# First stage of a graph layer: transposes ahead of the build, value sums ahead of weights, and ScalarE instead of GpSimd for one widening copy

## The chip, the cores and the metric

One core of one Trainium2 chip. The time is that of the whole program on the device, in microseconds (us). Engines: TensorE (PE in profiles, its weight loads PEld), VectorE (DVE), ScalarE (ACT), GpSimd (POOL), SyncE (SP, which only issues transfers here).

## The reference, cut to what matters

A layer on a graph of 3125 nodes and 53125 edges sorted by destination. Node features `x` (3125 x 256) are normalized to `xn`, and then:

```
h = spmm(xn)                       # sum over edges of weight * xn[dst], into row src
z = spmm(h);  a0 = softmax(z @ W0.T + b0);  z = spmm([a0, a0]);  a1 = softmax(z @ W1.T + b1)
x = x + tanh(concat(a0, a1) + h) + mix(xn)    # mix: linear attention, k and v = layernorm(xn @ wk.T), (xn @ wv.T)
x = x + ffn(layernorm(x))                     # 8 experts, top 1, fixed capacity
```

The kernel never gathers edges. It turns the edge list into the dense adjacency matrix (25 x 25 tiles of 128 x 128) by matrix products of one-hot rows, stores it, and applies it three times. The change lies in the first stage, where edges are sorted into tiles, keys and values are projected, and the first strip of the matrix is built.

## The kernel before, in words

Each engine runs one list of instructions in order; engines wait for each other at semaphores. A loop of `it` = 0, 1, ... is written out on four engines. For `it` up to 24 it handles one tile of 128 nodes per pass and, a few passes later, one *unit* (four 128 x 128 blocks of the matrix: rows of tile u, columns of tiles 0 to 3). These first 25 passes are the first stage. What stands in pass `it`:

- **TensorE**, in this order: `product(it)` (keys and values of a node tile, L1654), `ranks(it)` (three matmuls that count edges per slot, L1628 to L1630), `build(it-3)` (the blocks of a unit, L1676), `slots(it-1)` (18 matmuls that put a tile's edges into slots, L1640), `kvprod(it-5)` (L1661), `turn(it+1)` (two transposes of the next node tile for the next `product`, L1587), `apply(it-4)` (a unit times the features, L1697).
- **ScalarE**: `turned(it)` (L819, the transposed tile from PSUM to `XT`), `weigh(it-3)` (L848, the unit's four row one-hots times their edge weights), in passes 1, 5 and 15 `cast` (L813 to L815), `normal(it+3)` (L806), in every fifth pass a square root of head variances (L898), `paired(it)` (L836), `squares(it)` (L825 copies the product out, L828 sums squares per head), `evac(it-3)` (L861, the built unit from PSUM; after every fifth unit it also issues a store, L865), `kept(it-1)` (L840, the slots' records from PSUM to `recs`).
- **VectorE**: in passes 2, 6 and 16 `prepare` (a group of tiles' edge fields), `spread(it)` (L1105, and the scan L1107), in every fifth pass `head_var` (L1129, waits for `squares(it-1)`), `slot(it-1)` (L1114 reads the ranks, L1117 makes one-hots, L1122 the payload), in every fifth pass `head_scale` (L1134 to L1138, waits for ScalarE's root), `normed(it-5)` (L1145), `hots(it-2)` (L1165, a unit's row and column one-hots `eq_b` in bf16).
- **GpSimd**: in passes 1, 5 and 15 `pieces` (L686 to L690), weights of tile it-1 out of `recs` (L700, L702, semaphore `s_wsum`), the value sum of tile it-6 (L707, `s_vsum`), and the widening of unit it-2's column one-hots from bf16 to f32, `lead_col` (L712, semaphore `s_wide`). L702 and L707 add, L712 copies 128 x 512 elements.

One PSUM bank, `MISC`, holds the slots' records in its first part and the transposed tile in its second; the semaphores around it are `s_slotted` and `s_recrd` (`kept` done), `s_turned` and `s_xt` (`turned` done). From pass 25 on, VectorE builds the one-hots alone in bf16, and a pass on TensorE is `build` and `apply`.

Of the kernel before, what the change touches and what calls it, by code (L numbers as in the profile page):

```python
# [18 lines left out]
P = 128  # L19
NT = 25  # L20
# [40 lines left out]
LEAD = NT  # L61
# [65 lines left out]
def hot_free(u):  # L127
    return u - 2 if u < LEAD + 3 else u - 3


KV_LAG = 5
# [18 lines left out]
def graph_program(nc, a, out):  # L150
    ctx = ExitStack()
    with ctx:
# [3 lines left out]
        def sem(name):  # L156
            return ctx.enter_context(nc.semaphore(name))
# [230 lines left out]
        s_eq = sem("s_eq")  # L388
        s_hot = sem("s_hot")
        s_wgt = sem("s_wgt")  # L390
        s_wide = sem("s_wide")
        s_bmm = sem("s_bmm")
        s_bev = sem("s_bev")
        s_app = sem("s_app")
# [256 lines left out]
        def _(gp):  # L651
# [40 lines left out]
            for it in range(NT + KV_LAG + 1):  # L692
                if it in CAST_AT:
                    pieces(CAST_AT[it])
                if 1 <= it <= NT:
                    j = it - 1
                    w1, w2, w3 = (recs[:, j, 0:6:5, f, :] for f in (2, 3, 4))
                    whole = lead_w[:, j * 8:(j + 1) * 8].rearrange("p (g q) -> p g q", g=2)
                    gp.wait_ge(s_recrd, j + 1)
                    gp.tensor_tensor(whole, w1, w2, ALU.add).then_inc(s_wpart, 1)  # L700
                    gp.wait_ge(s_wpart, j + 1)
                    gp.tensor_tensor(whole, whole, w3, ALU.add).then_inc(s_wsum, 1)  # L702
                if it > KV_LAG:
                    m = it - KV_LAG - 1
                    gp.wait_ge(s_khat, m + 1)
                    ge(gp, s_vsum, m)
                    gp.tensor_tensor(vacc.rearrange("p (c n) -> p c n", c=2), vacc.rearrange("p (c n) -> p c n", c=2), khat[m % 2][:, 2:4, 0:P], ALU.add).then_inc(s_vsum, 1)  # L707
                u = it - HOT_IT
                if 0 <= u < LEAD:
                    gp.wait_ge(s_hot, u + 1)  # L710
                    ge(gp, s_bmm, hot_free(u))
                    gp.tensor_copy(lead_col[hot_of(u)], eq_b[u % 2][:, 1].rearrange("p c k i -> p c i k")).then_inc(s_wide, 1)  # L712

            gp.wait_ge(s_m, 1)
            gp.memset(blank, 0.0).then_inc(s_blank, 1)
# [57 lines left out]
        def _(act):  # L773
# [47 lines left out]
            def squares(m):  # L821
                g, i = m // KT, m % KT
                act.wait_ge(s_prod, m + 1)
                ge(act, s_khat, m - 5)
                nc.scalar.copy(KC[m % 6], ps[:, PROD, :])  # L825
                ge(act, s_sq, m)
                for h in range(NH):
                    head = nc.scalar.activation(sq[:, h * HD:(h + 1) * HD], ps[:, PROD, h * HD:(h + 1) * HD], ACT.Square,  # L828
                                                accum_out=hvar[:, g % 2, i * NH + h:i * NH + h + 1])
                head.then_inc(s_sq, 1)  # L830
# [11 lines left out]
            def weigh(u):  # L842
                act.wait_ge(s_hot, u + 1)
                act.wait_ge(s_wsum, u + 1)
                ge(act, s_bmm, hot_free(u))
                h = hot_of(u)
                for i, (j, s) in enumerate(UNITS[u]):
                    last = nc.scalar.activation(lead_row[h][:, i // 2, i % 2, :], eq_b[u % 2][:, 0, i // 2, :, i % 2], ACT.Copy, scale=lead_w[:, j * 8 + s:j * 8 + s + 1])  # L848
                    if j == s:
                        own = nc.scalar.activation(lead_own[h][:, 0, :], lead_own[h][:, 0, :], ACT.Copy, scale=lead_w[:, j * 8 + 7:j * 8 + 8])  # L850
                        last = own
                last.then_inc(s_wgt, 1)
# [26 lines left out]
            x_rows(2)  # L879
            x_rows(3)  # L880
            for it in range(NU + 3):
                if it < NT:
                    turned(it)
                if it == 1:
                    for to, src in ((wo_n, half("L0_mix_wo")), (wq_n, half("L0_mix_wq")), (W0_n, a["L0_gnn_W0"]),
                                    (W1_n, a["L0_gnn_W1"]), (b1_n, a["L0_ffn_b1"])):
                        act.dma_start(to, src).then_inc(s_wt5, 16)
                u = it - BUILD_IT
                if 0 <= u < LEAD:
                    weigh(u)  # L890
                if it in CAST_AT:
                    cast(CAST_AT[it])
                if it + 3 < NT:
                    normal(it + 3)
                if it in range(KT, NT + 1, KT):
                    g = it // KT - 1
                    act.wait_ge(s_hvar, g + 1)
                    nc.scalar.activation(hrs[:, g % 2, :], hvar[:, g % 2, :], ACT.Sqrt).then_inc(s_hroot, 1)  # L898
                if it < NT:
                    paired(it)  # L900
                    squares(it)
                if it == 2:
                    roots(1)
                if 0 <= u < NU:
                    evac(u)
                    if u - 1 in [strip_end(k) for k in range(NS)]:
                        strip_out(strip_of(u - 1))
                if 1 <= it <= NT:
                    kept(it - 1)
                if it == 2:  # L910
                    others_out()
# [92 lines left out]
        def _(dve):  # L1004
# [143 lines left out]
            def hots(u):  # L1148
# [6 lines left out]
                if u < LEAD:  # L1155
# [4 lines left out]
                        for a in range(2):  # L1160
                            v.tensor_scalar(lead_own[h][:, a, :], iota_n[:, :], rec(t, SPARE, a), None, ALU.is_equal)
                    ge(dve, s_wgt, u - 1)
                    ge(dve, s_wide, u - 1)
                    fields = recs[:, j, 0, 0:2, :].rearrange("p f (c i) -> p f c i", i=2)
                    v.tensor_tensor(eq_b[u % 2], every.unsqueeze(1).unsqueeze(1).to_broadcast([P, 2, 2, P, 2]),  # L1165
                                    fields.unsqueeze(3).to_broadcast([P, 2, 2, P, 2]), ALU.is_equal).then_inc(s_hot, 1)
# [417 lines left out]
        def _(pe):  # L1584
# [47 lines left out]
            def slots(j):  # L1632

                b = j % 2
                k = ohk[b].rearrange("p (c k i) -> p c k i", k=P, i=2)
                p = V[:, b, :].rearrange("p (c f s i) -> p c f s i", f=5, s=NR, i=2)
                pe.wait_ge(s_pay, j + 1)
                ge(pe, s_recrd, j)
                for c in range(WC):
                    last = nc.tensor.matmul(ps[:, MISC, 0:140].rearrange("p (f s) -> p f s", f=5)[:, :, 0:NR], k[:, c // 2, :, c % 2], p[:, c // 2, :, :, c % 2], start=(c == 0), stop=(c == WC - 1))  # L1640
                last.then_inc(s_slotted, 1)

            def turn(m):
                pe.wait_ge(s_xn, m + 1)
                ge(pe, s_xt, m)
                ge(pe, s_recrd, m - 1)
                flip(ps[:, MISC, D:D + P], XN[:, m, 0:P])
                flip(ps[:, MISC, D + P:2 * D], XN[:, m, P:2 * P]).then_inc(s_turned, 1)

# [14 lines left out]
            def build(u):  # L1664
# [2 lines left out]
                piece = lambda a, i, w: pair_b[h][:, a, i // 2, 0:w, i % 2]  # L1667
                ge(pe, s_bev, u - 1)
                pe.wait_ge(s_wgt if u < LEAD else s_hot, u + 1)
                if u < LEAD:  # L1670
                    pe.wait_ge(s_wide, u + 1)
                for i, (j, s) in enumerate(UNITS[u]):
                    c = width(t for _, t in UNITS[u][:i])
                    w = width([s])
# [50 lines left out]
            for it in range(NU + 4):  # L1725
                if it < NT:
                    product(it)
                if it < NT:
                    ranks(it)
                if it == 2:  # L1730
                    others()
                if it == APPLY_IT:
# [10 lines left out]
                    slots(it - 1)  # L1743
                if KV_LAG <= it < NT + KV_LAG:
                    kvprod(it - KV_LAG)
                if it + 1 < NT:
                    turn(it + 1)
                if it == NT + KV_LAG:
                    pe.wait_ge(s_vsum, NT)
                    pe.wait_ge(s_sq, NT)  # L1750
# [260 lines left out]
```

## Time and profile before

| | us |
|---|---|
| median of 3 runs (lowest, highest) | 1113.7 (1112.21, 1114.81) |
| profiled execution, its own time | 1114.14 |
| span of its profile | 1112.4 |
| TensorE busy in the span | 1063.1 (96%) |
| VectorE busy | 716.0 (64%) |
| ScalarE busy | 313.7 (28%) |
| GpSimd busy | 199.1 (18%) |

The shares are means over the whole program; the first stage ends near 212 us. In a row of the timeline the first number is the start in us from the beginning of the span, the second the duration; a bracket at the end gives the idle time of the engine before the row and what ended it. A matmul's start in the timeline can lie up to 0.2 us before its place in the chain of waits, since matmuls overlap.

### The profile page before, as it was taken

How to read it: one execution, taken by the hardware profiler on the slowest of the kernel's cores; microseconds unless marked ns; L12 is line 12 of the kernel's file. 1: busy time of each engine (PE TensorE's matmuls, PEld its weight loads, DVE VectorE, ACT ScalarE, POOL GpSimd, SP SyncE). 2: the span in 40 equal slices, each digit the busy share in tenths (PEclk: the TensorE clock that was granted, in tenths of full speed). 3: DMA queues.
4: the chain of work that ended last, by engine and by line, in shares of the span. 5: the costliest groups of instructions: out<-in, count | busy, mean ns of one | idle time of the engine just before them, and what ended most of it. 6: DMA issues, size and time to landing. Idle time of an engine off the chain costs nothing.

```text
span 1112.4 us, 15255 instructions
## 1 busy us (share of the span) xinstructions
PE 1063.1 (96%) x5391; PEld 664.0 (60%) x5391; DVE 716.0 (64%) x1611; ACT 313.7 (28%) x1042; POOL 199.1 (18%) x243
## 2 busy tenths in 40 slices
PE   5899999999999999999999999999998899999995
PEld 3466566666566665566784444644457566666664
DVE  8999999897775876869840111237777554444444
ACT  4777777322212222222211111211112221222220
POOL 2234454400101010110000000000443511111111
PEclk9999999999999999999999999999999999999998
DMA  6120011123333333423259988897994686555510
GB/s 178 19 58 13 37 49 48 49 95 134 133 134 133 134 133 133 166 110 143 96 203 365 366 311 304 342 329 280 311 323 156 184 223 142 134 134 138 140 39 8
DMA packets 80986, 178.58 MB, mean 161 GB/s; under 512 B 35678, under 2 KB 64122, under 8 KB 68750
## 3 DMA queue, kind: packets, MB, share of 16 engines
q1 hardware_dynamic: 67592, 123.39, 34.8%
q10 hardware_dynamic: 9190, 46.12, 10.5%
q0 software_dynamic: 4128, 8.08, 2.1%
q8 instruction: 45, 0.74, 0.3%
q14 instruction: 31, 0.25, 0.1%
HBM read 116.23 MB, written 63.77 MB: 162 GB/s over the span
## 4 chain that ended last, share of the span: by engine, by line
PE 83%; DVE 9%; ACT 3%; issue 2%; another core or an unknown queue 1%; DMA 1%; POOL 0%; SPq 0%; ACTq 0%; POOLq 0%; DVEq 0%
PE ps L1697 23%; PE ps L1851 20%; PE ps L1976 10%; PE ps L1964 9%; PE ps L1681 7%; PE ps L1654 2%; PE ps L1720 2%; PE ps L1587 2%; PE ps L1640 2%; PE ps L1676 1%; ACT W L828 1%; DVE XT L1487 1%; DVE W L1122 1%; PE ps L1661 1%
## 5 line engine op out<-in xcount | busy, mean ns | idle before, releaser
L1697 PE MATMUL ps<-RING,XX 128*128 128x512 f32 (+2 forms) x700 | 296.2, 548 | 1.6 <-DVE W L1194 1.6
L1851 PE MATMUL ps<-RING,RY 128*128 128x512 f32 (+4 forms) x750 | 271.3, 518 | 1.4 <-issue 1.4
L1851 PEld LDWEIGHTS ps<-RING,RY 128*128 128x128 f32 x750 | 135.0, 192 | 121.3 <-issue 113.6
L861 ACT COPY RING<-ps 128x512 f32<-128x512 f32 (+3 forms) x163 | 92.3, 566 | 279.0 <-PE ps L1681 259.7
L1697 PEld LDWEIGHTS ps<-RING,XX 128*128 128x128 f32 x700 | 117.5, 190 | 68.9 <-issue 61.6
L1187 DVE TENSOR_TENSOR RING<-RING,RY 128x1536 bf16<-128x1536 bf16 (+1 forms) x150 | 140.0, 940 | 4.0
L1681 PEld LDWEIGHTS ps<-RING 128*128 128x128 bf16 x1575 | 100.6, 97 | 52.0 <-issue 46.4
L1177 DVE TENSOR_TENSOR RING<-iota_p,RY 128x1024 bf16<-128x1024 bf16 (+1 forms) x150 | 96.8, 652 | 29.0 <-PE ps L1681 26.5
L1681 PE MATMUL ps<-RING 128*128 128x128 bf16 (+1 forms) x1575 | 112.9, 217 | 0.0
L998 ACT ACTIVATE RY<-ps,b1T 128x489 f32<-128x489 f32 x64 | 42.8, 669 | 164.9 <-PE ps L1964 162.0
L1554 DVE SCALAR_TENSOR_TENSOR W<-ps,RING,W 128x256 f32<-128x256 f32 (+1 forms) x32 | 15.5, 484 | 90.8 <-PE ps L1976 89.7
L1365 DVE TENSOR_REDUCE nmx<-ps 128x4 f32<-128x512 f32 (+2 forms) x7 | 4.4, 634 | 103.8 <-PE ps L1587 103.8
L724 POOL TENSOR_TENSOR XX<-XX,bo_b 128x256 f32<-128x256 f32 x25 | 27.5, 1100 | 232.9 <-PE ps L1681 232.8
L768 POOL DMA_INDIRECT out<-W,RING x32 | 31.3, 979 | 182.2 <-DVE W L1561 160.1
L1976 PE MATMUL ps<-XT,RY 128*128 128x256 f32 (+1 forms) x256 | 55.9, 379 | 0.0
L1976 PE MATMUL ps<-RING,RY 128*128 128x256 f32 (+1 forms) x256 | 55.9, 379 | 0.0
L1964 PE MATMUL ps<-RING,XT 128*128 128x489 f32 x128 | 53.3, 574 | 0.0
L1964 PE MATMUL ps<-RING 128*128 128x489 f32 x128 | 53.1, 573 | 0.0
L1654 PE MATMUL ps<-wkvT,XT 128*128 128x512 f32 x100 | 48.7, 611 | 4.5 <-ACT XT L819 4.5
L1976 PEld LDWEIGHTS ps<-XT,RY 128*128 128x128 f32 (+1 forms) x256 | 47.4, 185 | 9.3 <-issue 1.8
L1976 PEld LDWEIGHTS ps<-RING,RY 128*128 128x128 f32 (+1 forms) x256 | 47.4, 185 | 9.3 <-issue 1.8
L743 POOL DMA_INDIRECT xbuf_dram<-XX,sidx x25 | 25.1, 1003 | 118.9 <-DVE sidx L1475 112.1
(287 smaller groups left out, 1332.5 us busy)
## 6 DMA issues: line engine op xcount, KB each, us to landing
RING<-adj_dram SPq DMA_DIRECT2D x60, 1280.0 KB
adj_dram<-RING ACTq DMA_DIRECT2D x30, 1280.0 KB, 4.8
rbuf_dram<-W SPq DMA_DIRECT2D x8, 516.0 KB, 5.2
RING<-rbuf_dram SPq DMA_DIRECT2D x8, 516.0 KB, 4.0
xbuf_dram<-W SPq DMA_DIRECT2D x8, 512.0 KB, 3.3
XT<-in_L_ffn_w SPq DMA_DIRECT2D x16, 256.0 KB
XT<-in_L_ffn_w SPq DMA_DIRECT2D x4, 1024.0 KB
RING<-in_L_ffn_w SPq DMA_DIRECT2D x16, 256.0 KB
```

What stands on the lines that cost most here:

```text
L724: gp.tensor_tensor(X1[:, j, :], X1[:, j, :], bo_b[:, :], ALU.add).then_inc(s_bo, 1)
L768: gp.indirect_dma_start(out[:, :], bass.IndirectOffsetOnAxis(ap=rbs[0:n, e % 2, c, D + 1:RES].bitcast(I32), axis=0), ybs[0:n, e % 2, c, :] ...
L861: nc.scalar.copy(RING[:, n % 2, at:at + w], ps[:, u % 2, 0:w]).then_inc(s_bev, 1)
L998: nc.scalar.activation(hmT[:, f, 0:CAPX], ps[:, 2 + f % 3, 0:CAPX], ACT.Relu, bias=b1T[:, f, e:e + 1]).then_inc(s_hidv, 1)
L1177: last = v.tensor_tensor(to[:, 0:4:3], every.unsqueeze(1).unsqueeze(1).to_broadcast([P, 2, c, P, 2]), fields[:, 0:2].unsqueeze(3).to_broad ...
L1187: last = v.tensor_tensor(to[:, 1:4], to[:, 3:4].to_broadcast([P, 3, c, P, 2]), fields[:, 2:5].unsqueeze(3).to_broadcast([P, 3, c, P, 2]), ...
L1654: last = nc.tensor.matmul(ps[:, PROD, :], XT[:, c, m * P:(m + 1) * P], wkvT[:, c, :], start=(c == 0), stop=(c == 1))
L1681: last = nc.tensor.matmul(o[:, c:c + w], piece(0, i, P), piece(1 + f, i, w), start=(f == 0), stop=(f == 2 and j != s))
L1697: last = nc.tensor.matmul(ps[:, ACC + dd, 0:w], XN[:, j, dd * H:(dd + 1) * H], at[:, i * w:(i + 1) * w], start=(j == 0), stop=True, skip_g ...
L1851: last = nc.tensor.matmul(o, (Y if l == 0 else S0)[:, j, :], RING[:, slot_of[g % 5], i * across + first:i * across + first + w], start=(j ...
L1964: last = nc.tensor.matmul(ps[:, 2 + f % 3, 0:CAPX], w1s[s][:, c, f * P:(f + 1) * P], xbT[:, s, c, 0:CAPX], start=(c == 0), stop=(c == 1))
L1976: last = nc.tensor.matmul(o, hmT[:, f, c * P:c * P + n], w2s[s][:, f, :], start=(f == 0), stop=(f == 7))
```

## The change

Four edits. (1) On TensorE `turn(it+1)` stands behind `ranks(it)` instead of behind `kvprod`; it waits for the records of one tile earlier (`s_recrd` m-2 instead of m-1), and `slots(it-1)` gets a wait for `turned(it+1)`, because both use `MISC`. (2) On ScalarE `turned(it+1)` moves from the head of the next pass into `squares(it)`, behind the copy L825. (3) On GpSimd the value sum stands ahead of the weights. (4) The widening copy leaves GpSimd and becomes the first instruction of `weigh` on ScalarE; `s_wide` goes, on VectorE and TensorE too.

```
@@ gpsimd, loop over it
                 if it in CAST_AT:
                     pieces(CAST_AT[it])
+                if it > KV_LAG:
+                    m = it - KV_LAG - 1
+                    gp.wait_ge(s_khat, m + 1)
+                    ge(gp, s_vsum, m)
+                    gp.tensor_tensor(vacc..., vacc..., khat[m % 2][:, 2:4, 0:P], ALU.add).then_inc(s_vsum, 1)
                 if 1 <= it <= NT:
...
-                if it > KV_LAG:
...
-                u = it - HOT_IT
-                if 0 <= u < LEAD:
-                    gp.wait_ge(s_hot, u + 1)
-                    ge(gp, s_bmm, hot_free(u))
-                    gp.tensor_copy(lead_col[hot_of(u)], eq_b[u % 2][:, 1].rearrange("p c k i -> p c i k")).then_inc(s_wide, 1)
@@ scalar, squares(m)
                 nc.scalar.copy(KC[m % 6], ps[:, PROD, :])
+                if m + 1 < NT:
+                    turned(m + 1)
@@ scalar, weigh(u)
                 h = hot_of(u)
+                nc.scalar.copy(lead_col[h], eq_b[u % 2][:, 1].rearrange("p c k i -> p c i k"))
                 for i, (j, s) in enumerate(UNITS[u]):
@@ scalar, loop over it
-                if it < NT:
-                    turned(it)
+                if it == 0:
+                    turned(0)
@@ vector, hots(u)
                     ge(dve, s_wgt, u - 1)
-                    ge(dve, s_wide, u - 1)
@@ tensor, slots(j)
                 ge(pe, s_recrd, j)
+                pe.wait_ge(s_xt, min(j + 3, NT))
@@ tensor, turn(m)
                 ge(pe, s_xt, m)
-                ge(pe, s_recrd, m - 1)
+                ge(pe, s_recrd, m - 2)
@@ tensor, build(u)
-                if u < LEAD:
-                    pe.wait_ge(s_wide, u + 1)
@@ tensor, loop over it
                 if it < NT:
                     ranks(it)
+                if it + 1 < NT:
+                    turn(it + 1)
...
                     kvprod(it - KV_LAG)
-                if it + 1 < NT:
-                    turn(it + 1)
```

TensorE, one whole pass of the steady part, before, from `product` to `apply`:

```order
L1654 MATMUL ps<-wkvT,XT 128x512 x2
L1628 MATMUL ps<-HB,before 128x468
L1629 MATMUL ps<-HB,ident_b 128x468
L1630 MATMUL ps<-HB,own_b 128x468
L1676 MATMUL ps<-RING 128x128 x4
L1640 MATMUL ps<-W,RY 128x5x26 x18
L1661 MATMUL ps<-W 128x129 x2
L1587 MATMUL ps<-ident,XX 128x128 x2
L1697 MATMUL ps<-RING,XX 128x512 x2
```

The same pass now (line numbers are those of the changed kernel):

```order
L1651 MATMUL ps<-wkvT,XT 128x512 x2
L1624 MATMUL ps<-HB,before 128x468
L1625 MATMUL ps<-HB,ident_b 128x468
L1626 MATMUL ps<-HB,own_b 128x468
L1583 MATMUL ps<-ident,XX 128x128 x2
L1671 MATMUL ps<-RING 128x128 x4
L1637 MATMUL ps<-W,RY 128x5x26 x18
L1658 MATMUL ps<-W 128x129 x2
L1692 MATMUL ps<-RING,XX 128x512 x2
```

The two transposes (`ps<-ident,XX`) have moved past the build, the slots and `kvprod`; nothing else has changed place.

ScalarE, one pass of the steady part, before, from `turned` to `kept`:

```order
L819 COPY XT<-ps 128x2x128
L848 ACTIVATE RING<-RING,RY 128x128 x4
L806 ACTIVATE XX<-XX,mvx,lnr 128x256
L836 COPY HB<-HB 128x26x9x2
L825 COPY RING<-ps 128x512
L828 ACTIVATE W,hvar<-ps 128x64 x8
L861 COPY RING<-ps 128x512
L840 CAST RY<-ps 128x140
```

And now:

```order
L843 CAST RING<-RING 128x512
L845 ACTIVATE RING<-RING,RY 128x128 x4
L800 ACTIVATE XX<-XX,mvx,lnr 128x256
L832 COPY HB<-HB 128x26x9x2
L819 COPY RING<-ps 128x512
L813 COPY XT<-ps 128x2x128
L824 ACTIVATE W,hvar<-ps 128x64 x8
L858 COPY RING<-ps 128x512
L836 CAST RY<-ps 128x140
```

The copy to `XT` now stands between the copy of the product and the squares, and a cast of 128 x 512 (the widening) opens the pass.

GpSimd around pass 15, before (the three `HB<-HB` rows are `pieces`):

```order
L712 CAST RING<-RING 128x512 [waits s_bmm,s_hot]
L686 TENSOR_TENSOR HB<-HB 128x162 [waits s_cast]
L688 CAST HB<-HB 128x81x2 [waits s_piece]
L690 TENSOR_TENSOR HB<-HB 128x81x2 [waits s_piece]
L700 TENSOR_TENSOR RY<-RY 128x8 [waits s_recrd]
L702 TENSOR_TENSOR RY<-RY 128x8 [waits s_wpart]
L707 TENSOR_TENSOR RY<-RY,W 128x256 [waits s_vsum,s_khat]
```

And now:

```order
L685 TENSOR_TENSOR HB<-HB 128x162 [waits s_cast]
L687 CAST HB<-HB 128x81x2 [waits s_piece]
L689 TENSOR_TENSOR HB<-HB 128x81x2 [waits s_piece]
L698 TENSOR_TENSOR RY<-RY,W 128x256 [waits s_vsum,s_khat]
L704 TENSOR_TENSOR RY<-RY 128x8 [waits s_recrd]
L706 TENSOR_TENSOR RY<-RY 128x8 [waits s_wpart]
```

The value sum (`RY<-RY,W`) no longer stands behind a wait for `s_recrd`, and the widening is gone.

## Rows read from the trace of the kernel before

**Rows 1.** Busy time of each engine in three stretches (start:end, length, busy by engine)

```profile
20.00:60.00 40.00, 31.28 (x191) 19.59 (x192) 38.81 (x84) 28.23 (x142) 8.78 (x20) 0.91 0.23 37
216.00:850.00 634.00, 629.47 (x3315) 375.48 (x3315) 385.06 (x894) 116.66 (x269) 55.02 (x54) 1.00 0.56 208
```

**Rows 2.** Chain that ended last, one pass near 90 us (start, us, what)

```profile
89.67 1.72 PE ps L1697 x4
91.39 1.72 PE ps L1654 x4
93.10 0.20 PE ps L1628
...
93.70 0.89 PE ps L1676 x8
94.59 1.08 PE ps L1640 x18
95.67 0.50 PE ps L1661 x4
...
96.17 0.41 PE ps L1587 x2
```

**Rows 3.** TensorE's waits, 65 to 216 us (us in total, times, longest)

```profile
PE ps L1676 <- POOL RING L712: 2.2, 1, 2.2
PE ps L1587 <- ACT RY L840: 2.1, 4, 0.5
PE ps L1640 <- DVE W L1122: 1.7, 2, 0.9
PE ps L1628 <- DVE HB L1114: 1.5, 1, 1.5
```

**Rows 4.** Timeline of ScalarE behind the issue of a store

```profile
110.09 0.28 ACT L840 CAST RY<-ps 128x140 bf16<-128x140 f32 x1 [0.42 <-ACT RING L861]
```

**Rows 5.** Timeline of ScalarE in a steady pass

```profile
103.53 0.37 ACT L819 COPY XT<-ps 128x256 f32<-128x256 f32 x1 [0.59 <-PE ps L1587]
...
105.47 0.63 ACT L836 COPY HB<-HB 128x468 bf16<-128x468 bf16 x1
106.96 0.59 ACT L825 COPY RING<-ps 128x512 f32<-128x512 f32 x1 [0.87 <-PE ps L1654]
```

**Rows 6.** Timeline of GpSimd and VectorE: a value sum, a payload, and one whole VectorE pass

```profile
89.63 1.82 POOL L707 TENSOR_TENSOR RY<-RY,W 128x256 f32<-128x256 f32 x1
...
90.82 1.86 DVE L1122 TENSOR_TENSOR W<-HB 128x2340 bf16<-128x2340 bf16 x1
...
108.81 1.13 DVE L1107 TENSOR_TENSOR_SCAN HB<-HB 128x468 bf16<-128x468 bf16 x1
...
113.81 1.00 DVE L1145 TENSOR_TENSOR W<-RING,hrs 128x512 f32<-128x512 f32 x1 [0.65 <-POOL RY L707]
...
115.76 1.13 DVE L1107 TENSOR_TENSOR_SCAN HB<-HB 128x468 bf16<-128x468 bf16 x1
```

**Rows 7.** Timeline of TensorE and VectorE around passes 14 to 16

```profile
119.39 1.88 PE L1654 MATMUL ps<-wkvT,XT 128*128 128x512 f32 x4
...
123.75 0.16 DVE L1129 TENSOR_SCALAR hvar<-hvar 128x40 f32<-128x40 f32 x1
...
127.66 0.40 DVE L1134 RECIPROCAL hta<-hrs 128x40 f32<-128x40 f32 x1 [0.52 <-ACT hrs L898]
...
134.82 1.13 DVE L1107 TENSOR_TENSOR_SCAN HB<-HB 128x468 bf16<-128x468 bf16 x1
...
137.80 1.37 DVE L1122 TENSOR_TENSOR W<-HB 128x2340 bf16<-128x2340 bf16 x1
```

**Rows 8.** Timeline of TensorE and VectorE at the end of the stage, passes 24 and 25

```profile
198.54 1.38 DVE L1122 TENSOR_TENSOR W<-HB 128x2340 bf16<-128x2340 bf16 x1
...
201.76 0.69 DVE L1145 TENSOR_TENSOR W<-RING,hrs 128x512 f32<-128x512 f32 x1
...
203.22 0.66 PE L1661 MATMUL ps<-W 128*128 128x129 f32 x4
```

More of the change, by code:

```diff
@@ L390, in graph_program @@
         s_wgt = sem("s_wgt")
-        s_wide = sem("s_wide")
         s_bmm = sem("s_bmm")
@@ L694, in _ @@
                     pieces(CAST_AT[it])
+                if it > KV_LAG:
+                    m = it - KV_LAG - 1
+                    gp.wait_ge(s_khat, m + 1)
+                    ge(gp, s_vsum, m)
+                    gp.tensor_tensor(vacc.rearrange("p (c n) -> p c n", c=2), vacc.rearrange("p (c n) -> p c n", c=2), khat[m % 2][:, 2:4, 0:P], ALU.add).then_inc(s_vsum, 1)
                 if 1 <= it <= NT:
@@ L702, in _ @@
                     gp.tensor_tensor(whole, whole, w3, ALU.add).then_inc(s_wsum, 1)
-                if it > KV_LAG:
[L704 to L707, printed above, removed]
-                u = it - HOT_IT
-                if 0 <= u < LEAD:
-                    gp.wait_ge(s_hot, u + 1)
-                    ge(gp, s_bmm, hot_free(u))
-                    gp.tensor_copy(lead_col[hot_of(u)], eq_b[u % 2][:, 1].rearrange("p c k i -> p c i k")).then_inc(s_wide, 1)
             gp.wait_ge(s_m, 1)
```

## Prediction

> **What bounds the kernel now.** I read four views in this order: busy time by stretch, the chain that ended last, TensorE's waits, and the timeline around the longest of them.
>
> Busy time by stretch divides the program in three. From 20 to 60 us VectorE is busy 38.81 of 40 us while TensorE is busy 31.28: there VectorE sets the pace. From 216 to 850 us TensorE is busy 629.47 of 634 us [rows 1], so whatever the first stage saves or loses is handed on whole to the end. The change can only win between about 60 and 216 us.
>
> The chain of one pass near 90 us lies on TensorE alone: 1.72 (`apply`) + 1.72 (`product`) + 3 x 0.20 (`ranks`) + 0.89 (`build`) + 1.08 (`slots`) + 0.50 (`kvprod`) + 0.41 (`turn`) = 6.92 us [rows 2]. The change leaves that sum as it is; it can only take away waits. Between 65 and 216 us these are 2.2 + 2.1 + 1.7 + 1.5 = 7.5 us [rows 3], which bounds the gain from above. They are of three kinds: four times 0.5 us at `turn`, which waits for `kept`; 1.7 and 1.5 us for VectorE, in two places, pass 6 and pass 16, where `prepare` has lengthened its pass; and once 2.2 us for GpSimd's widening at the end of the stage.
>
> **Edits 1 and 2, the turn.** The four waits of 0.5 us come where `kept` stands behind the issue of a store and waits 0.42 us more [rows 4]. Now `turn(it+1)` waits for `kept` of one tile earlier, which ended a pass ago, so all four go: 2.1 us at most. Stores come every fifth pass, so two of the four lie before pass 16 (7 and 12) and two behind it (17 and 22). What the edit costs: `slots` now needs the copy of `turned`. After the product's end `ranks` and `turn` take 0.6 + 0.41 = 1.0 us, the copy to `XT` is 0.37 us [rows 5], so it is there at about 1.5 us. TensorE reaches `slots` at 0.6 + 0.41 + 0.89 = 1.9 us: covered by the build, with 0.4 us to spare. Without that cover each pass would lose up to the whole copy.
>
> The wait of pass 6 (the 0.8 us that the two in the list leave beside the longest, 0.9) stands at `slots(5)`. The payload that it waits for comes from VectorE, which has no gap there, so its time stays. But the 0.41 us of `turn` now run inside this wait instead of behind it: TensorE starts `product(7)` **0.4 us** earlier.
>
> **Edit 4, the widening on ScalarE.** ScalarE's nearest row is a permuted copy of 468 bf16 elements, 0.63 us [rows 5]; with the overlap of neighbours it holds the engine some 0.5 us, and I take 0.55. In a steady pass ScalarE is idle 0.59 + 0.87 = 1.46 us [rows 5], so it fits, with 0.9 us left, 0.5 where a store is issued. Bounds: nothing, and 1.82 us, the longest GpSimd instruction shown [rows 6], if ScalarE were that slow (I give this little: a copy of 128 x 512 from PSUM takes ScalarE 0.59 us [rows 5]).
>
> **Edit 3 and VectorE's pace.** A VectorE pass without disturbance: from scan to scan 115.76 - 108.81 = 6.95 us, less the 0.65 us that it waits for the value sum, less 0.31 by which `normed` is long there (1.00 against 0.69) [rows 6, 8], gives 6.0 us. A value sum that meets VectorE's work costs the instruction behind it 0.48 us (the payload at 90.82 took 1.86 us, with 1.38 elsewhere, while the sum ended at 91.45) [rows 6, 8]. Before, a pass paid for a value sum and for a widening; now only for the sum, which comes just behind `normed` and so meets `hots` and `spread`. `head_scale` adds some 1.8 us in five passes (payload's end 199.92 to `normed` 201.76) [rows 8]. So VectorE needs 6.0 + 0.48 + 0.36 = 6.84 us against TensorE's 6.92. TensorE keeps the pace, but with little to spare: the sum holds as long as a value sum costs VectorE under 0.56 us in a pass.
>
> **Pass 16.** By then TensorE is 0.4 + 2 x 0.5 = 1.4 us ahead of before Can it keep this? `prepare` makes it wait twice (1.5 and 0.9 us), so VectorE sets the time there. VectorE in turn waited 0.52 us for ScalarE's root at 127.66, which is 6.4 us after the end of `product(14)` at 121.27 [rows 7]. On that path ScalarE now has the widening more (0.55); the wait for `turn` only changes its place. So the root comes 1.4 - 0.55 = 0.85 us earlier, and with it scan and payload (137.80 + 1.37 = 139.17 before), and `slots(15)`. Behind `slots` there is no `turn` any more: 0.41. That gives 1.26 us at `product(17)`. Between reciprocal and scan lie 7.16 us [rows 7] in which GpSimd's widenings no longer disturb VectorE; this is worth between 0 and 2 x 0.48 us, and I take 0.25, since the `pieces` still stand there. Sum up to `product(17)`: **1.5 us** (1.25 to 2.2). In other words: of the 1.4 us collected nothing is added here, because the root moves with the product.
>
> **Passes 17 to 24**: the other two waits at `turn`, **1.0 us**.
>
> **End of the stage.** The 2.2 us at `build(22)` come because the widening stands on GpSimd behind a value sum. On ScalarE it follows `kept(23)`, 0.28 us, and with `weigh`'s four rows (under 1.6 us, since `turned` at 103.53 and `paired` at 105.47 leave 1.94 for more than that [rows 5]) it is done at most 2.4 us behind `slots(23)`; TensorE meanwhile has `kvprod` and `apply`, 0.50 + 1.72 = 2.2 us. So this wait goes but for 0.2 us. What is late next: `kvprod(20)`. It started at 203.22; without the wait TensorE would be there at 201.0. But it needs `normed(20)`, which ended at 202.45, after a payload that ended at 199.92, a `head_scale` and 0.69 us [rows 8]. VectorE did not stand behind the 2.2 us, so this chain does not move by itself: 203.22 - 202.5 = 0.7 us. If `head_scale` shrinks by what GpSimd took, it is up to 1.1. I take **0.9 us**.
>
> **The sum.** 1.5 + 1.0 + 0.9 = 3.4 us. Against the profiled execution: 1114.1 - 3.4 = 1110.7 us. That execution is 0.4 us above the median of the runs shown, so the forecast is 1110.3 us. A change under 0.2% (2.2 us) is about what a measurement of this kernel can't tell from none.
>
> **The rivals.**
>
> *A. The value sum costs VectorE more, and VectorE takes over the pace (slower).* Place: `hots`, `spread` and scan behind `normed`. If each value sum lengthens two instructions instead of one, it costs 0.96 us; VectorE then needs 7.32 us a pass, 0.40 over TensorE, in the 17 passes from 7 to 24 that is 6.8 us. 3.4 are won, so 3.4 us slower: 1117.1. The change turns into a loss from 0.56 + 3.4 / 17 = 0.76 us a pass. For it: the margin is only 0.08 us. Against it: the scan has 1.13 us in every row shown [rows 6, 7], disturbed or not. The Trainium skill, "GPSIMD Engine Reference", section 1 "Specifications", says that GpSimd shares its SBUF interfaces with VectorE, with contention where a VectorE instruction reads two SBUF inputs. All the instructions behind `normed` are of that kind, so by that rule the cost moves with the value sum and does not go. The rows agree as far as the payload goes, and no row bears out two hits by one sum. Chance 0.07.
>
> *B. Less is won.* The root of pass 15 is later than I take it (widening and cast stand in a row ahead of it), so that of the 1.4 us only the 0.4 of `turn` remains, and at the end `kvprod` gains nothing. Then 0.4 + 1.0 = 1.4 us, up to 2.2: about 1112.0. For it: both places hang on chains that TensorE's reordering does not shorten. Chance 0.19.
>
> *C. More is won.* VectorE, freed of the widening, gets far enough ahead that the 2.4 us of pass 16 and the 2.2 us of the end both shrink to little. The upper bound is 7.5 us; with half of pass 16 and 2.0 at the end it is 1.4 + 0.4 + 1.2 + 1.0 + 2.0 = 6.0 us: 1107.7. Against it: the two waits for ScalarE (root, `squares`) tie VectorE to the product. Chance 0.08.
>
> *D. ScalarE becomes the bound (slower).* If the widening held it over the 1.46 us that it is idle, `turned` would be late and `slots` with it. From 1.46 + 3.4 / 17 = 1.66 us on the gain is gone; at 1.82 us it would be 17 x 0.36 = 6.1 us more than forecast, 1116.4. Against it: no ScalarE row of this size is half as slow. Chance 0.02.
>
> **How the numbers follow.** My forecast, 2.3 to 5 us won, has the remaining 0.64. Its own range is 1108.6 to 1111.5. Faster by over 0.2%: 0.64, C's 0.08 and a small part of B, 0.02: 0.74. Within 0.2%: the rest of B, 0.17. Slower: A and D, 0.09. The range takes in C's 1107.7 below and B's 1112.0 with some of the runs' own scatter (2.6 us between lowest and highest) above, and leaves A and D out: 1107.5 to 1112.8.
>
> **What would show it.** Right: no wait of TensorE for `kept` at `turn` between 65 and 200 us; passes 8 to 15 each 6.92 us from product to product; `product(7)` 0.4 us earlier; pass 16 still with two waits for VectorE of together 2 us or more; at the end a wait at `kvprod` for VectorE in place of that at `build`; ScalarE's idle time a pass down from 1.46 to about 0.9 us; payloads of 1.37 us throughout, and lengthened `hots` or `spread` instead. The forecast is wrong if TensorE waits for VectorE's payload in passes 8 to 15 (A), if it waits for `turned` at `slots` (D), or if the root of pass 15 does not come earlier (B).

## The result, and the profile after

| us | before | changed |
|---|---|---|
| median of 5 runs | 1113.7 (1112.21 to 1114.81) | 1106.12 (1103.93 to 1107.23) |
| ratio to before, 95% interval | | 0.9931 (0.9916 to 0.9947) |
| profiled execution, its own time | 1114.14 | 1103.93 |
| span of its profile | 1112.4 | 1102.2 |

The kernel became 7.6 us faster (1113.7 - 1106.12). The forecast was 3.4 us, with a range down to 1107.5: faster is right, the size is not.

First, where the time came from. The table takes the start of one piece of TensorE's work in both timelines; a negative number is earlier than before.

| start of | before | changed | difference | change since the row above |
|---|---|---|---|---|
| `product(7)` | 69.96 | 69.92 | -0.04 | |
| `product(15)` | 126.30 | 123.75 | -2.55 | -2.51 |
| `product(17)` | 142.92 | 139.86 | -3.06 | -0.51 |
| `product(24)` | 192.31 | 186.98 | -5.33 | -2.27 |
| first strip of the second `spmm` | 579.69 | 573.17 | -6.52 | -1.19 |
| the same work near 830 us | 830.14 | 823.55 | -6.59 | -0.07 |
| end of the span | 1112.39 | 1102.18 | -10.20 | -3.6 |

The first stage gave 6.5 us, and they are handed on whole as far as 830 us, as forecast. The last 3.6 us come behind 830 us, where the change touches nothing; an experiment below puts half of them down to TensorE's clock. The medians, 7.6 us apart, lie nearer to the first stage's gain.

Busy time by stretch (start:end, length, busy time by engine PE, PEld, DVE, ACT, POOL, then granted clock), changed kernel, and last the second of these stretches before:

```profile
20.00:60.00 40.00, 30.99 (x195) 19.75 (x196) 38.83 (x86) 31.54 (x156) 8.40 (x17) 0.96 0.22 37
60.00:216.00 156.00, 150.13 (x956) 99.45 (x955) 148.61 (x201) 120.95 (x534) 56.54 (x67) 0.99 0.12 45
216.00:850.00 634.00, 630.43 (x3335) 378.71 (x3333) 384.16 (x909) 118.40 (x275) 60.55 (x59) 1.00 0.57 212
```

```profile
60.00:216.00 156.00, 147.21 (x921) 96.22 (x919) 147.31 (x189) 110.16 (x515) 74.49 (x89) 1.00 0.12 45
```

The first and third rows answer to [rows 1] and are as before: VectorE full at the start, TensorE full from 216 us. Between them TensorE and VectorE were equally full; now TensorE is a little fuller (150.13 of 156 us against 148.61). ScalarE has taken over work (120.95 us against 110.16) and GpSimd has given it up (56.54 against 74.49).

TensorE's waits of the changed kernel from 65 to 216 us (us in total, times, longest), to be held against [rows 3]:

```profile
PE ps L1624 <- DVE HB L1111: 1.6, 1, 1.6
PE ps L1658 <- DVE W L1142: 1.0, 1, 1.0
PE ps L1637 <- DVE W L1119: 0.7, 1, 0.7
PE ps L1671 <- ACT RING L845: 0.3, 1, 0.3
```

They sum to 3.6 us, against 7.5 before. So 3.9 us of waits went, close to the 3.4 that were forecast: none for `kept` at `turn` is left, none for GpSimd, and `kvprod` waits for `normed` (1.0) in place of `build`. That is not enough for 6.5 us. The chain that ended last (the work and the waits that the end of the program hung on) shows the rest. One whole pass of the changed kernel, beside [rows 2]:

```profile
90.27 1.72 PE ps L1651 x4
91.99 0.20 PE ps L1624
...
92.58 0.22 PE ps L1583 x2
92.80 0.89 PE ps L1671 x8
93.69 1.09 PE ps L1637 x18
94.78 0.50 PE ps L1658 x4
95.28 1.72 PE ps L1692 x4
96.99 1.72 PE ps L1651 x4
```

A pass takes 96.99 - 90.27 = 6.72 us, against 6.92. Every piece has the length that it had but one: `turn`, the two transposes, takes 0.22 us where it took 0.41. Over passes 7 to 24 the starts of the products show the same: 6.72 to 6.74 us from one to the next in the changed kernel, 6.91 or 6.92 before (7.42 to 7.44 where a store was issued), pass 16 apart. So 16 passes each gave about 0.18 us that stood in no list of TensorE's waits.

**Where it hid in the trace of before.** The same two transposes, on the row of the weight loads. The answer for that line, 60 to 200 us, of the kernel before ("sat idle" is the idle time of the weight-load row ahead of it, in total and how often):

```profile
L1587 PEld LDWEIGHTS ps<-ident,XX x36: 138/141/145, 68.0 to 190.4; 128*128 128x128 f32 x36
its engine sat idle before it (us, times) until:
  issue: 4.2, 13
```

On the row of the matmuls the list has 2.1 us for this line, four times [rows 3]. The weight loads have 13 waits and 4.2 us: the four of 0.5 are 0.67 to 0.69 here, and nine more have 0.16 or 0.17. In the changed kernel no idle time is listed ahead of that line. One of the nine, and one of the four, each behind ScalarE's `kept` of the same pass, all before:

```profile
95.71 0.32 ACT L840 CAST RY<-ps 128x140 bf16<-128x140 f32 x1
```

```profile
75.02 0.28 ACT L840 CAST RY<-ps 128x140 bf16<-128x140 f32 x1 [0.43 <-ACT RING L861]
```

```profile
95.45 0.52 PEld L1661 LDWEIGHTS ps<-W 128*128 128x128 f32 x4
96.14 0.20 PEld L1587 LDWEIGHTS ps<-ident,XX 128*128 128x128 f32 x2 [0.17 <-issue]
```

```profile
75.41 0.20 PEld L1587 LDWEIGHTS ps<-ident,XX 128*128 128x128 f32 x2 [0.69 <-issue]
```

`kept` ends at 95.71 + 0.32 = 96.03 and at 75.02 + 0.28 = 75.30, and the weight load starts 0.11 us later both times. It is so in every pass of that trace from 67 to 191 us: the first weight load of `turn` starts 0.10 to 0.12 us after `kept` has ended, whatever idle time stands ahead of it. So `turn` waited for `kept` in all of them. The matmuls of `kvprod` run on until 96.17 by the chain [rows 2], so TensorE's matmul row shows no gap at 96; the delay appears only as a `turn` that seems to take 0.41.

### The profile page after: what moved, and what is told of

Read it like the earlier page. It is cut to its first block, busy times and chain, and to the rows that moved or that the text cites. A ratio compares the mean times of both kernels' runs of the same rounds, so it can differ in the third digit from the quotient of the medians.

```text
span 1102.2 us, 15231 instructions
## 1 busy us (share of the span) xinstructions
PE 1057.2 (96%) x5391; PEld 662.0 (60%) x5391; DVE 710.7 (64%) x1611; ACT 327.0 (30%) x1067; POOL 181.0 (16%) x218
## 4 chain that ended last, share of the span: by engine, by line
PE 84%; DVE 10%; issue 2%; ACT 2%; DMA 1%; POOLq 0%; DVEq 0%; ACTq 0%
PE ps L1692 23%; PE ps L1846 20%; PE ps L1971 10%; PE ps L1959 10%; PE ps L1676 8%; PE ps L1651 2%; PE ps L1715 2%; PE ps L1637 2%; PE ps L1671 1%; PE ps L1583 1%; PE ps L1658 1%; DVE W L1119 1%; DVE bst L1232 1%; DMA XX<-in_x 1%; DVE XT L1483 1%
## 5 line engine op out<-in xcount | busy, mean ns | idle before, releaser
L1846 PE MATMUL ps<-RING,RY 128*128 128x512 f32 (+4 forms) x750 | 268.6, 514 | 0.1
```

Of the source, the lines that this page charges most:

```text
L1846: last = nc.tensor.matmul(o, (Y if l == 0 else S0)[:, j, :], RING[:, slot_of[g % 5], i * across + first:i * across + first + w], start=(j ...
```

## The experiments

Two theories stood for the 0.19 us a pass. **W (hidden wait):** `turn` waited for `kept` in every pass, not in four; the 0.41 us are 0.22 of work and 0.19 of waiting. **P (place):** nothing waited; two f32 transposes behind the f32 matmuls of `kvprod` cost 0.41 us, and behind the bf16 matmuls of `ranks` 0.22. Beside that it was open which of the four edits are needed. All kernels were timed in five rounds beside the kernel before. The last column is the change, against before, of the time from `product(7)` to the first strip of the second `spmm` in the profile (before 579.69 - 69.96 = 509.73 us): the first stage without its start, which differs by the clock from one execution to the next. Between these two points the clock was full throughout in ten of the twelve profiles, and low for a while in `e_turn` and `e_half`, as told there.

| kernel | median, us | ratio to before (95%) | `product(7)` to strip, us |
|---|---|---|---|
| changed kernel | 1106.12 | 0.9931 (0.9916 to 0.9947) | -6.48 |
| e_early: changed, `turn` ahead of `ranks` | 1104.6 | 0.9916 (0.9896 to 0.9936) | -6.54 |
| e_half: before, `turn` inside `apply` | 1109.79 | 0.995 (0.9931 to 0.9969) | -2.44 |
| e_turn: edits 1, 2 | 1114.02 | 1.0004 (0.9992 to 1.0017) | +0.60 |
| e_vsum: edit 3 | 1113.05 | 1.0003 (0.9984 to 1.0021) | -1.13 |
| e_widen: edit 4 | 1112.58 | 0.9994 (0.998 to 1.0008) | -1.09 |
| e_nowiden: edits 1, 2, 3 | 1110.85 | 0.9961 (0.9947 to 0.9976) | -3.13 |
| e_novsum: edits 1, 2, 4 | 1107.6 | 0.993 (0.9908 to 0.9952) | -6.25 |
| e_after2: changed, again | 1106.89 | 0.994 (0.9916 to 0.9964) | -6.45 |
| e_best: changed, with two more moves | 1104.81 | 0.991 (0.9891 to 0.9928) | -7.68 |
| e_best2: the same again | 1104.57 | 0.9926 (0.9902 to 0.9951) | -7.72 |

### e_early: the transposes behind f32 matmuls, without the wait

```
@@ changed kernel, tensor, loop over it
                     product(it)
-                if it < NT:
-                    ranks(it)
                 if it + 1 < NT:
                     turn(it + 1)
+                if it < NT:
+                    ranks(it)
```

> The changed kernel with the two transposes of turn put one place further up, directly behind product and ahead of ranks. Theory W (a hidden wait): before, each turn waited some 0.19 us for kept without the wait showing as idle time, so any place without that wait gives 0.22 us for the pair and 6.73 us for a pass, and the whole is within 1 us of the changed kernel (ratio to before 0.993). Theory P (the place): the pair costs 0.41 us behind f32 matmuls (kvprod before, product here) and 0.22 us only behind the bf16 ranks; then a pass is 6.92 us again and, over 17 passes, some 3 us are lost against the changed kernel (ratio 0.996).

Its chain, one pass:

```profile
96.20 1.72 PE ps L1651 x4
97.92 0.22 PE ps L1583 x2
98.13 0.20 PE ps L1624
```

Behind the f32 matmuls of `product` the transposes also take 0.22 us, and a pass takes 102.92 - 96.20 = 6.72 us. P in the form that f32 matmuls ahead make them long falls. The time is as good as that of the changed kernel: the place is free, as long as it lies behind nothing that comes late.

### e_half: the wait of before, met later in the pass

```
@@ kernel before, tensor, apply(u): turn between its two pairs of matmuls
                     for dd in range(2):
+                        if dd == 1 and between is not None:
+                            turn(between)
@@ loop over it
-                if it + 1 < NT:
+                if it + 1 < NT and it < APPLY_IT:
                     turn(it + 1)
...
-                    apply(it - APPLY_IT)
+                    apply(it - APPLY_IT, it + 1 if it + 1 < NT else None)
```

> Before, with turn in the middle of apply (behind its first two of four matmul passes) instead of ahead of it; its wait for kept stays as it was, and GpSimd and ScalarE keep their order. Theory W: kept is done 0.86 us earlier relative to turn, so turn costs 0.22 us instead of 0.41, passes 8 to 15 take 6.73 us, and the four waits of 0.5 us shrink to nothing or near it; the widening has 0.9 us of room on GpSimd, so no new wait at build. 3 to 5 us won by the first stage (ratio 0.996). Theory P: the pair keeps 0.41 us behind an f32 matmul, only the four waits go, 1 to 2 us won. Rival to both: VectorE, with value sum and widening still on GpSimd, needs 6.8 to 7 us a pass and TensorE waits for it; then under 1 us is won.

Its chain around one `turn`:

```profile
96.75 0.86 PE ps L1699 x2
97.61 0.22 PE ps L1587 x2
97.83 0.86 PE ps L1699 x2
```

All four edits are absent and the semaphores are those of before; `turn` is only 0.86 us later in the pass, when `kept` is done. It takes 0.22 us, most passes take 6.72, and no wait for `kept` stands in the list. (Behind a store the first weight load of `turn` still starts 0.11 us after `kept`, but those passes, too, take 6.72 or 6.73.) The new semaphore value and the other edits are thus not needed for the 0.22, and with the fixed 0.11 us behind `kept` in the trace of before this speaks for W: what counts is whether `kept` has ended. A kernel that only relaxes the wait and leaves the order as it was, with `turn` directly behind `kvprod`, wasn't tried.

The gain is smaller than the change's. The 2.2 us for GpSimd's widening at the end stay. Six passes take 6.83 to 7.27 us; of that the list names only two new waits for the widening, of 0.2 and 0.3 us (with the 2.2 they are 2.7 in three), and the rest was not traced. The ranks of pass 16 wait 2.0 us for VectorE, where they waited 1.5. And in pass 16, from 137 to 140 us, TensorE's clock was low: `slots` takes 1.82 us there in the chain instead of 1.08.

### e_turn, e_vsum, e_widen: the edits one by one

`e_turn` is the kernel before with the hunks of edits 1 and 2 of the diff above, `e_vsum` with that of edit 3, `e_widen` with those of edit 4, nothing else.

> Before with edits 1 and 2 alone (turn ahead of the build, turned inside squares); GpSimd keeps its order and the widening. Theory W and P both: 6.73 us a pass if TensorE sets the pace. But VectorE still pays for a value sum and a widening in each pass: 6.0 + 2 x 0.48 + 0.36 = 7.3 us at most, so I expect it to take over, with passes of 6.9 to 7.1 us, TensorE waiting for L1122 or L1114 in several passes, and 1 to 3 us won. Rival: the edits on GpSimd do nothing by themselves, and this kernel wins the whole 6 us.

> Before with edit 3 alone (value sum ahead of the weights on GpSimd). Turn still waits: passes of 6.92 us. VectorE no longer waits 0.65 us for the value sum. At the end the widening stands behind the weights only, so the wait at build(22) falls from 2.2 us to about 1 us: 0 to 1 us won. Rival: value sum and widening both collide with VectorE behind normed, passes lengthen, and 1 to 2 us are lost.

> Before with edit 4 alone (widening on ScalarE). Turn still waits for kept: passes of 6.92 us, the four waits of 0.5 us stay. The wait of 2.2 us at build(22) goes and comes back in part at kvprod(20); payloads of 1.86 us become 1.37 us. 0.5 to 1.5 us won. Rival: ScalarE, 0.5 us fuller, makes kept later and with it turn: passes over 7.0 us and a loss of 1 to 3 us.

None of the three can be told from no change by its time. In `e_turn`, for which 1 to 3 us were expected, 9 of the 17 passes have 6.72 to 6.74 us, but much of that is given back. Its waits, and its chain near 92 us and in pass 16:

```profile
PE ps L1679 <- POOL RING L712: 4.8, 8, 2.2
```

```profile
89.98 0.36 ACT RY L842
...
90.42 0.20 POOL RY L700
...
90.77 1.26 issue
92.03 1.82 POOL RY L707
93.85 0.56 POOL RING L712
94.41 0.14 issue
94.54 1.13 PE ps L1679 x8
...
138.66 1.71 PE ps L1679 x8
140.37 1.73 PE ps L1643 x18
```

GpSimd's list runs in order: the weights (L700, L702) wait for `kept`, the value sum of 1.82 us stands behind them, and the widening, whose operands come from VectorE and not from `kept`, stands behind both. `build` waits for it eight times, 4.8 us in all: the 2.2 us at the end, as before, and seven new waits of together 2.6 us. A faster pass on TensorE has made the GpSimd queue the next bound; VectorE, which was expected to take over, stands in the same list with 2.1 us in pass 16 and 0.5 us in pass 6 only.

The +0.60 of this profile holds more than its waits. TensorE's clock was low twice for 3.4 us between `product(7)` and the strip, once behind the 2.1 us in pass 16 (granted 0.57 and 0.58 from 138 to 142 us), once behind the 2.2 us at the end of the stage (0.50 from 204 to 206 us). The last two rows above are `build` and `slots` of pass 16, which take 0.89 and 1.08 us at the full clock. The longer `build` costs nothing, since `slots` has to wait for VectorE's payload (138.73 + 1.37 = 140.10) in any case; the longer `slots` costs 0.65 us. At the end `slots`, `kvprod` and `apply` are together 1.6 us longer. Without these 2.3 us the column would read about -1.7, an estimate. The median of 12 executions shows no gain all the same, and why is open.

In `e_widen` the four waits at `turn` stay (2.1 us) and passes take 6.91; at the end the 2.2 us for the widening become 0.9 at `kvprod` and 0.3 at `build`. In `e_vsum` passes take 6.92, and the wait at `build` shrinks from 2.2 to 1.6 us.

### e_nowiden and e_novsum: which partner the turn needs

`e_nowiden` has edits 1, 2 and 3 and leaves the widening on GpSimd; `e_novsum` is the changed kernel with the value sum back behind the weights.

```
@@ changed kernel, gpsimd (e_novsum)
-                if it > KV_LAG:
-                    m = it - KV_LAG - 1
...
                     gp.tensor_tensor(whole, whole, w3, ALU.add).then_inc(s_wsum, 1)
+                if it > KV_LAG:
+                    m = it - KV_LAG - 1
```

> Edits 1, 2 and 3: the changed kernel with the widening left on GpSimd, now behind the weights only. Theory Q (queue on GpSimd): what eats the turn's gain without edits 3 and 4 is that kept comes later and weights, value sum and widening stand behind it in a row; without the value sum in that row (1.8 us) the widening is done in time, waits of TensorE for L712 disappear or are under 0.5 us in all until the end of the stage, and 3 to 5.5 us of the 6.5 are won. Theory V (VectorE): its collisions with two GpSimd instructions a pass are what eats the gain; then TensorE waits for VectorE, passes are 6.9 to 7.0 us, and under 2 us are won.

> Edits 1, 2 and 4: the changed kernel with the value sum behind the weights as before. Theory Q: the widening is off GpSimd, so nothing that build needs stands behind the value sum; passes of 6.73 us, VectorE waits for the value sum in some passes (0.6 us each) but has the room; 5 to 6.5 us won, within 1 us of the changed kernel. Theory V: the same, since one GpSimd instruction is gone. If instead VectorE's waits for the value sum reach TensorE, 2 to 4 us are won.

With edits 1 and 2 in place, the last column of the table reads +0.60 alone, -3.13 with edit 3, -6.25 with edit 4 and -6.45 or -6.48 with both. Edit 3 shortens the queue ahead of the widening. The 3.7 us between the first two numbers are not all its own: the first has the 2.3 us of low clock told above, and in the second TensorE is idle for 1.2 us right ahead of the strip (at 578.19 us), for which the profile shows no cause and which none of the other profiles has. Without both, the two would be near -1.7 and -4.4, and edit 3 worth some 2.7 us as long as the widening stands on GpSimd; the times, 1.0004 and 0.9961 with intervals apart, bear out that it is worth something there. Once the widening is gone, edit 3 is worth some 0.2 us in the profile and nothing that the times can tell (1107.6 against 1106.12 and 1106.89, with intervals that overlap). In `e_novsum` VectorE waits for the value sum seven times, 5.3 us in all, and TensorE's waits hardly change: those waits lie off the path. In `e_nowiden` what is left is 4.8 us for VectorE's ranks, in two (2.7 us of it ahead of `product(7)`), and 1.6 us for the widening at the end.

### e_best, e_after2, e_best2: a faster version, and the clock

```
@@ changed kernel: the last group's cast and pieces in pass 11, not 15
-CAST_AT = {t0 - 1: g for t0, g in PREPARE_AT.items()}
+CAST_AT = {t0 - 1 if g < 3 else 11: g for t0, g in PREPARE_AT.items()}
@@ vector: head_var behind the slot's one-hots, not ahead of the ranks
-            def slot(j):
+            def slot(j, turn=False):
...
                                 rk.rearrange("p (c i) -> p c i", i=2)...
+                if turn:
+                    head_var((j + 1) // KT - 1)
...
-                if turn:
-                    head_var(it // KT - 1)
...
-                    slot(it - 1)
+                    slot(it - 1, turn)
```

> The changed kernel, with head_var moved behind the one-hots of slot (it waited 0.8, 0.4 and 1.5 us for squares in passes 10, 15 and 25) and with cast and pieces of the last group in pass 11 instead of 15 (so that neither stands ahead of ScalarE's root in pass 15). If those waits hold VectorE's lead down, the two waits of TensorE in pass 16 fall from 2.3 us to about 1 and the 1.0 us at kvprod(20) goes: 1.5 to 2.5 us faster than the changed kernel (ratio to before 0.991). If VectorE's plain work sets pass 16, the waits there stay over 2 us and only the last 1 us is won.

> The changed kernel once more, on the same chip as e_best2. Theory W puts 6.5 us of its gain in the first stage; the rest of the 10.2 us between the two profiles lies behind 840 us, where the changed kernel's profile has no half-clock stretch and that of before has one. If that part is chance, this run's profile either has such a stretch (then about 1.7 us longer behind 840 us) or not, and the ratio to before stays between 0.992 and 0.995.

> e_best once more, beside the changed kernel on one chip: its first stage again about 2 us shorter, ratio to before 0.002 under that of e_after2.

TensorE's waits of `e_best`, 65 to 216 us:

```profile
PE ps L1637 <- DVE W L1121: 1.2, 2, 0.7
PE ps L1624 <- DVE HB L1111: 1.2, 1, 1.2
```

The wait at `kvprod` is gone and that for the ranks in pass 16 is shorter (1.2 us against 1.6). From `product(7)` on the two profiles of it are 1.2 us shorter than those of the changed kernel, where 1.5 to 2.5 us were expected; the medians of `e_best2` and `e_after2`, timed together, are 1104.57 against 1106.89, with intervals against before that overlap. It is faster than before beyond doubt, and than the changed kernel by about 1 us in the profile, which the times alone don't settle.

The repeated kernel also tells what the clock does. Granted clock (third number from the end, as a share of the full clock) in three stretches, first the changed kernel, then the same kernel again:

```profile
64.00:68.00 4.00, 4.00 (x32) 0.59 0.15 14
855.00:860.00 5.00, 3.81 (x29) 1.00 0.15 53
860.00:865.00 5.00, 4.76 (x20) 1.00 0.46 113
```

```profile
64.00:68.00 4.00, 3.50 (x35) 1.00 0.13 12
855.00:860.00 5.00, 4.53 (x26) 0.65 0.16 55
860.00:865.00 5.00, 5.00 (x11) 0.67 0.53 118
```

One program, and TensorE runs for most of 64 to 68 us at the lower of its two levels (1.2 instead of 2.4 GHz) in one execution, and for part of 855 to 865 us in the other. Before's profile had it at 860 to 865 us (0.74). From the work near 830 us to the end, the profiles without such a stretch take 278.6 or 278.7 us (the changed kernel, `e_novsum`, `e_best`); with one short stretch 280.3 or 280.4 (`e_early`, `e_widen`, `e_vsum`, `e_half`, `e_nowiden`, `e_best2`), `e_after2`, with a stretch twice as long, 280.6; and `e_turn`, with one three times as long (0.53 and 0.50 from 865 to 875 us), 282.3. That is 1.7 us and more, with the edits and without them. Before had one short stretch and took 282.3. So of the last 3.6 us in the first table 1.7 are the clock's. The other 1.9 belong to the one profile of before, where TensorE also has small waits there (1.4 us in four at the matmuls of the last strips, 0.8 at two transposes) that are in none of the other profiles, those of `e_vsum` and `e_widen`, with before's order on TensorE, included. What caused them is open; the first stage's order does not explain them.

## Why the prediction was wrong in size, and what of it held

**The step that failed** is in its second paragraph: "The chain of one pass near 90 us lies on TensorE alone: ... = 6.92 us. The change leaves that sum as it is; it can only take away waits", and the bound of 7.5 us drawn from it. It read the 0.41 us of `turn` as work. 0.19 of it were a wait for `kept`, as the weight loads of before show, with `e_half` and `e_early` beside them. The sum of a pass was 6.72 us of work, and its waits were not 7.5 but about 7.5 + 16 x 0.18 = 10.4 us. Set term against term:

| stretch | forecast | measured | what makes the difference |
|---|---|---|---|
| 7 to 15 | -1.0 | -2.51 | 8 passes x 0.18 = 1.4 |
| 15 to 17 | -0.1 | -0.51 | pass 15: 0.18; pass 16: 0.34 shorter, below |
| 17 to 24 | -1.0 | -2.27 | 7 passes x 0.18 = 1.3 |
| from 24 on | -0.9 | -1.19 | 0.3 more at the end |
| sum | -3.0 | -6.48 | of 3.5 us, 2.9 are the hidden wait |

The evidence was there: `turned` [rows 5] waits for `turn`, `turn` came when `kept` ended, and the weight-load row listed 13 waits where TensorE's listed four. Rival C names a time nearer the result, 1107.7, but its mechanism, a freed VectorE that shrinks the waits of pass 16, is not what happened: they went from 2.4 us (1.5 and 0.9 in [rows 3]) to 2.3.

**Edits 1 and 2.** The four waits of 0.5 went, as forecast. That the build covers the copy to `XT` is right: no wait of TensorE for it is in the list. `product(7)` was forecast 0.4 us earlier and came 0.04 earlier, but with the low clock from 64 us on. In `e_after2`, without it, it came 0.97 earlier, of which 0.61 stand already in VectorE's work (scan of pass 7 at 67.16 against 67.77; what moved it is open); the remaining 0.36 are the forecast's term.

**Edit 4, edit 3 and VectorE.** One steady pass of the changed kernel, all engines:

```profile
107.49 1.13 DVE L1104 TENSOR_TENSOR_SCAN HB<-HB 128x468 bf16<-128x468 bf16 x1
...
109.39 0.62 ACT L843 CAST RING<-RING 128x512 f32<-128x512 bf16 x1
109.91 1.28 ACT L845 ACTIVATE RING<-RING,RY 128x128 f32<-128x128 bf16 x4
...
111.76 0.69 DVE L1142 TENSOR_TENSOR W<-RING,hrs 128x512 f32<-128x512 f32 x1
111.86 1.13 POOL L698 TENSOR_TENSOR RY<-RY,W 128x256 f32<-128x256 f32 x1
...
112.37 1.17 DVE L1161 TENSOR_TENSOR RING<-iota_p,RY 128x1024 bf16<-128x1024 bf16 x1
...
113.89 1.13 DVE L1104 TENSOR_TENSOR_SCAN HB<-HB 128x468 bf16<-128x468 bf16 x1
```

The widening holds ScalarE 109.91 - 109.39 = 0.52 us (taken: 0.55), and it fits: rival D is out. ScalarE's idle time is 0.55 + 0.22 = 0.77 us in the pass from 100 us on (taken: about 0.9). The value sum now begins inside `normed` (L1142), and the `hots` behind it take 1.17 us, elsewhere 0.68; in two of the passes from 7 to 15 it is the slot's one-hots (L1114) that are longer, 1.82 and 1.84 us against 1.36. The payload keeps 1.36 to 1.38, the scan 1.13. So one sum lengthens one instruction by 0.49 us, as taken (0.48), and rival A's double hit did not come. VectorE's pass is 113.89 - 107.49 = 6.40 us (taken: 6.0 + 0.48 where no `head_scale` stands), so it keeps 0.3 us ahead of the 6.72. The Trainium skill, "GPSIMD Engine Reference", section 1 "Specifications", has GpSimd share its SBUF interfaces with VectorE, with contention for VectorE instructions with two SBUF inputs. The trace agrees, with 1.17 us for `hots` beside the sum against 0.68: the cost moved with the value sum and did not go.

**Pass 16.** Two waits of TensorE for VectorE were to stay, of together 2 us or more. In the timeline of TensorE:

```profile
133.95 0.36 PE L1624 MATMUL ps<-HB,before 128*128 128x468 bf16 x1 [1.59 <-DVE HB L1111]
...
136.54 1.27 PE L1637 MATMUL ps<-W,RY 128*128 128x130 bf16 x18 [0.73 <-DVE W L1119]
```

They are 2.3 us. The path to them is VectorE's, which waits for ScalarE's root:

```profile
125.44 0.40 DVE L1131 RECIPROCAL hta<-hrs 128x40 f32<-128x40 f32 x1 [0.21 <-ACT hrs L895]
...
132.14 1.13 DVE L1104 TENSOR_TENSOR_SCAN HB<-HB 128x468 bf16<-128x468 bf16 x1
```

The reciprocal is 2.22 us earlier than in [rows 7], the scan 2.68. Product(14) was 2.36 earlier (117.03 against 119.39), so the widening cost this path 0.14 us and not the 0.55 taken; from reciprocal to scan 0.46 were won (taken 0.25, within 0 to 0.96). "The root moves with the product" was right; the product had moved further than thought.

**End of the stage.** As forecast, `kvprod` waits in place of `build`:

```profile
196.86 0.71 PE L1658 MATMUL ps<-W 128*128 128x129 f32 x4 [0.95 <-DVE W L1142]
```

0.3 us at `build` remain (taken 0.2). In all 1.19 us were won from `product(24)` on, against 0.9.

**What each edit is worth.** The forecast's terms were summed as if each edit brought its own. They don't add: edits 1 and 2 carry the gain, but only with the widening off GpSimd's queue. Edit 4 alone is worth 1.1 us in the profile; edits 1 and 2 alone some 1.7 by the estimate above, and nothing by the times; the three together 6.25. Edit 3 beside them adds almost nothing.

## What to carry to other kernels

Before you call a piece of a chain work, compare its length with the same instructions elsewhere, and read the weight-load row as well as the matmul row: a wait that ends while the matmuls ahead still run showed only there, and a fifth of a microsecond in each pass was nearly half of this gain. When you bound a gain by listed waits, add what recurs in every pass. And before you set two profiles against each other, look at the granted clock of the stretch between the points that you compare. When an engine's pass gets shorter, look at once for the in-order queue where an early-ready step stands behind a late one, because much of the gain can stop there.

## What the runs showed of the hardware that was not expected

The trace can hold a recurring wait without any idle time of the waiting engine: 0.19 us of `turn`'s 0.41, which began 0.11 us after the end of what it waited for. GpSimd's value sum took 1.82 us where it began 0.08 us behind the start of the slot's one-hots (89.55 to 90.91 us before, L1117; the sum in [rows 6]) and 1.13 where it began 0.10 behind the start of `normed`. Both times it ended 0.54 us behind the end of that instruction, which kept its length, and VectorE's next one was 0.48 or 0.49 us longer: the one that had begun first held the other up. And TensorE's lower clock level falls on one stretch in one execution and on another in the next: at 64 us in the changed kernel, after TensorE had waited 2.2 us, but not in the repeat, where it had waited as long; it made that pass 0.9 us longer (10.91 against 10.01 us from `product(6)` to `product(7)`).
